# Splitting the output weight during the attention, loading the next stage's weights in its last heads, and moving the weighted sums ahead of the projections

## Chip, cores and metric

One NeuronCore of a Trainium2 chip runs the whole program. The metric is the device time of one execution in microseconds (us), smaller being better. The kernel before takes 3414.24 us, the median of three runs (3413.55 to 3415.07).

## What is computed

The reference is one transformer-like layer on x of shape 8 x 512 x 1024 in float32 (cut):

```python
x = x + attn_a(layernorm(x))      # qkv = x @ qkvw + qkvb; 32 heads of 32; softmax(q k^T * scale) v; ctx @ ow + ob
x = x + ffn(layernorm(x))         # dots = softmax(x @ centroids.T / 0.1); hits = dots > 0.01
                                  # dense = x @ weight.T + bias, kept where a row's query and its cluster are hit
x = x + attn_b(layernorm(x))      # 4 heads of 256, sign-bound q, k, v, causal sigmoid scores
x = x + ffn(layernorm(x))
```

Every float32 product is made of three float16 products: each operand is scaled by a power of two and split into a high half `hi` and a rest `lo`; hi·hi, hi·lo and lo·hi are added in PSUM. A projection of 128 rows onto 512 columns over 1024 features is thus a unit of 24 matmuls (8 blocks of features, 3 products each).

## The kernel before, in words

The program has four stages, each a block of five instruction streams (PE, DVE, ACT, POOL, SP) that are synchronised by semaphores, with a barrier (`end_phase`) between stages. SP issues nearly all DMAs, in its own order.

Stage 0 splits the qkv weight into `wqk` and `wv`, which fill the arena (48 parts of 2 KB per partition; `wqk` is parts 0 to 32, `wv` parts 32 to 48).

Stage 1 is attention A. It walks over 256 heads (8 rows of the batch x 32 heads) in **slots** `s`; four consecutive slots are one **group** `m` (64 groups). A slot has four **steps** `c`. In each step PE issues, in this order: one matmul of the row maxima of head s+2 (`max_scores`, L484, into `ring_ps`), one matmul of the scores of head s (`scores`, L494, into `st_ps`), in most steps a quarter of a projection unit, 6 matmuls (`unit`, L533 for q and k, L543 for v, into `proj_ps`), and one quarter of the weighted sum of head s-2 (`weighted`, 8 small matmuls, L511 and L514, into `ctx_ps`). I call a step with a quarter unit *full* and one without *empty*. A group has 12 full and 4 empty steps: the first unit sits in steps 0 to 3, the next in 5 to 8, the third in 10 to 13. So the first step of a group's second slot is empty. From slot 240 on there are no v units (two units in a group), and from slot 248 on no units at all.

The other engines: DVE takes the row maxima (L652), copies the finished sums out of `ctx_ps` (`leave_ctx`, L678 and L679, at the first step of a slot), and makes the rest `elo` of the exponentials of the first half of the keys (L670). ACT makes each exponential twice (L592 to float32, L598 to float16 `ehi`) and copies `proj_ps` out (L607, L610). POOL makes `elo` of the second half (L758), the normalised context (L766, L772) and the halves of the projections (L811, L813). ACT may overwrite `e32` of the second half only after POOL's L758 of the head before. SP sends the row of maxima to the partition where the scores read it (`rows`, L439, `qs<-nrow`), stores and restacks q and k, and stores the context of each group (L443).

The output weight `ow` (4 MB) is loaded at slot 240 by four DMAs (L461), after the last v unit has freed its arena parts and ahead of that slot's `rows`. In slots 242 to 249 DVE takes its maximum (L702), in slot 249 POOL reduces it over the partitions (`partition_all_reduce`, L834), and after the last head ACT makes `hi` (L644, 8 instructions) and DVE `lo` (L749, 8 instructions).

Stage 2 adds the projected context: for each of 32 tiles, `turn_context` (L999, 8 transposes), `hi_context` on ACT (L1078) and `lo_context` on DVE (L1249), two units `project` (L1011) and a residual. Ahead of tile 0 stands `project_bias` (L975, 48 matmuls, the value bias times the output weight), for which ACT spreads `bv_hl` (L1099), and whose result DVE adds to `obias` (L1137) after the centroids' scale. Here SP also loads the output bias, the centroids, the assignments, the ffn bias and the 4 MB of the ffn weight (L937 to L942), and POOL reduces the centroids' maximum (L1305) before its first `biases` (L1312). A second reduction for the ffn weight stands ten tiles later (L1330). Stages 3 and 4 are not touched.

Of the kernel before, what the change touches and what calls it, by code (L numbers as in the profile page):

```python
# [28 lines left out]
P = 128  # L29
# [16 lines left out]
GH = 4  # L46
NC = 64
# [80 lines left out]
def hybrid_layer(nc, x, qkvw, qkvb, ow, ob, bvq, bvk, bvv, fw, fb, cent, assign, out):  # L128
# [8 lines left out]

    ctx_d = nc.dram_tensor("ctx_scratch", (B * G, T, P, P), F32).ap()
# [12 lines left out]
    with ExitStack() as top:  # L151
# [19 lines left out]
        e_v = sb(top, "e_v", [P, 1])  # L171
        s_v = sb(top, "s_v", [P, 1])
        e_o = sb(top, "e_o", [P, 1])
        bv_hl = sb(top, "bv_hl", [P, 2, C], F16)
# [8 lines left out]
        wo = part16(0, 16).rearrange("p (a c n) -> p a c n", a=2, c=C)  # L183
        ow_raw = part32(32, 48).rearrange("p (c n) -> p c n", c=C)
# [3 lines left out]
        with ExitStack() as p01:  # L188
# [3 lines left out]
            exp_scale = sb(p01, "exp_scale", [P, 1])  # L192

# [93 lines left out]
            with ExitStack() as p1:  # L287
# [16 lines left out]
                ow_in = [sem(f"ow_in{i}") for i in range(4)]  # L304
                bvT_in, omax_done, oall_done, osc_done, wo_hi, wo_lo, bv_done = (sem(n) for n in (
                    "bvT_in", "omax_done", "oall_done", "osc_done", "wo_hi", "wo_lo", "bv_done"))
# [99 lines left out]
                with nc.Block() as block:  # L406

                    @block.sync
                    def _(sp):
# [34 lines left out]

                        for t in range(FIRST):
                            sp.dma_start(x_first(t), x_t[t // T, t % T]).then_inc(x0_in[t], 16)
# [4 lines left out]
                        for s in SLOTS:  # L451
# [6 lines left out]
                            if s == OW_LOAD:  # L458
                                sp.wait_ge(proj_full, place["V", B - 1, T - 1, 1] + 1)
                                for j in range(4):  # L460
                                    sp.dma_start(ow_raw[:, 2 * j:2 * j + 2], ow.rearrange("(c p) n -> p c n", p=P)[:, 2 * j:2 * j + 2]).then_inc(ow_in[j], 16)  # L461
                                with nc.allow_non_contiguous_dma(reason="a small bias, one feature per partition"):
                                    sp.dma_start(bvT[:], qkvb[2 * H:3 * H].rearrange("(c p) -> p c", p=P)).then_inc(bvT_in, 16)
                            if i == 1:
                                store_parts(m + 2, 0)
                            rows(s + 2)
                            if i == 2:
                                store_parts(m + 2, 1)
# [4 lines left out]
                        for i in range(2):  # L473
                            sp.wait_ge(ctx_out[i], 16 * GROUPS // 2)

# [71 lines left out]

# [1465 lines left out]
```

## Time and profile before

| | us |
|---|---|
| median of 3 runs | 3414.24 |
| the profiled execution's own time | 3413.33 |
| span of its instructions | 3411.6 |
| PE busy | 3211.6 (94%) |
| DVE busy | 2173.1 (64%) |
| POOL busy | 1864.7 (55%) |
| ACT busy | 1776.3 (52%) |

Times below are in us from the start of the span. Stage 1 ends at 1916.8, stage 2 reaches from there to 2368. "Idle before it" in square brackets is how long the engine stood still before an instruction, and what ended that. PE's matmuls are pipelined: of a row of matmuls the distance between starts is the cost, and the duration shown is longer (0.38 us for 512 columns whose starts are 0.22 us apart at full clock).

### The profile page before, as it was taken

What the parts mean: (1) busy time and instruction counts of PE and PEld (TensorE: products, weight loads), DVE (VectorE), ACT (ScalarE), POOL (GpSimd) and SP (SyncE); (2) the same over time, 40 slices, a digit from 0 to 9 for tenths busy, and PEclk for the clock granted to TensorE, in tenths of its full rate; (3) what the DMA queues carried; (4) which work ended last, traced back from release to release, by engine and by line L of the source; (5) the groups of instructions that cost most, each with busy time, mean ns of one, the idle gap of its engine ahead of it and who ended that gap; (6) DMA issues with size and microseconds to landing.
All of it is one profiled execution on the core that took longest, in us unless ns stands there. A gap on an engine that the chain in (4) does not pass through costs nothing. (4 is left out here: it accounts for less than half of the span.)

```text
span 3411.6 us, 62568 instructions
## 1 busy us (share of the span) xinstructions
PE 3211.6 (94%) x24256; PEld 1705.5 (50%) x24256; DVE 2173.1 (64%) x3858; ACT 1776.3 (52%) x2125; POOL 1864.7 (55%) x2065
## 2 busy tenths in 40 slices
PE   0899999999999999999997699998999999999999
PEld 0355555555555555555553355554455555554443
DVE  8377777777777777777777587775455555542311
ACT  3277777777777777777775422221345555552000
POOL 2377777777777777777664322221555555540422
PEclk9999999999999999999997799999999999999999
DMA  4122222222222222222223454443222222213533
GB/s 185 41 60 72 64 71 72 71 69 66 69 64 72 63 76 69 69 70 59 59 59 100 159 168 159 154 163 119 79 81 99 100 100 104 95 75 142 198 141 136
DMA packets 272869, 330.36 MB, mean 97 GB/s; under 512 B 91677, under 2 KB 206365, under 8 KB 271551
## 3 DMA queue, kind: packets, MB, share of 16 engines
q1 hardware_dynamic: 267902, 309.57, 28.6%
q10 hardware_dynamic: 4608, 16.78, 1.2%
q8 instruction: 194, 3.18, 0.4%
q14 instruction: 101, 0.82, 0.1%
q0 software_dynamic: 64, 0.01, 0.0%
HBM read 191.52 MB, written 134.22 MB: 95 GB/s over the span
## 5 line engine op out<-in xcount | busy, mean ns | idle before, releaser
L652 DVE TENSOR_REDUCE nmax<-ring_ps 128x1 f32<-128x512 f32 x1024 | 686.8, 688 | 417.4 <-PE ring_ps L484 414.0
L758 POOL TENSOR_TENSOR elo<-e,ehi 128x1024 f16<-128x1024 f32 x256 | 615.9, 2406 | 432.5 <-ACT ehi L598 425.1
L533 PE MATMUL proj_ps<-xnT,arena 128*128 128x512 f16 x3072 | 750.2, 380 | 3.3 <-DVE xnT L697 2.5
L592 ACT ACTIVATE e<-st_ps,exp_scale 128x1024 f32<-128x1024 f32 x512 | 571.4, 1116 | 344.3 <-PE st_ps L494 260.9
L598 ACT ACTIVATE ehi<-st_ps,exp_scale 128x1024 f16<-128x1024 f32 x512 | 570.1, 1114 | 64.7 <-PE ctx_ps L514 57.1
L533 PEld LDWEIGHTS proj_ps<-xnT,arena 128*128 128x128 f16 x3072 | 299.5, 98 | 373.0 <-ACT stage L610 10.6
L1527 PE MATMUL f_ps<-wT,fxT 128*128 128x512 f16 x1920 | 434.3, 380 | 2.9 <-DMA fxT<-xT_scratch 2.9
L494 PE MATMUL st_ps<-qs,ks 98*128 98x512 f16 x1024 | 396.8, 387 | 16.6 <-ACT ehi L598 10.0
L511 PEld LDWEIGHTS ctx_ps<-v_sb,ehi 128*128 128x128 f16 x4096 | 313.6, 98 | 192.8 <-DVE sums L679 81.5
L484 PE MATMUL ring_ps<-ks,qs 96*128 96x512 f16 x1024 | 401.1, 392 | 8.4 <-DVE nmax L652 8.2
L511 PE MATMUL ctx_ps<-v_sb,ehi 128*128 128x65 f16 x4096 | 374.6, 193 | 30.6 <-DVE sums L679 20.7
L543 PE MATMUL proj_ps<-arena,xnT 128*128 128x512 f16 x1536 | 371.4, 378 | 2.8 <-ACT stage L610 2.1
L514 PE MATMUL ctx_ps<-v_sb,elo 128*128 128x33 f16 x4096 | 359.6, 180 | 0.0
L1011 PE MATMUL o_ps<-arena,cT 128*128 128x512 f16 x1536 | 344.0, 381 | 6.2 <-DVE cT L1249 6.2
L514 PEld LDWEIGHTS ctx_ps<-v_sb,elo 128*128 128x128 f16 x4096 | 276.6, 97 | 111.2 <-issue 6.0
L670 DVE TENSOR_TENSOR elo<-e,ehi 128x1024 f16<-128x1024 f32 x256 | 322.7, 1261 | 0.9 <-ACT ehi L598 0.9
L1527 PEld LDWEIGHTS f_ps<-wT,fxT 128*128 128x128 f16 x1920 | 187.1, 98 | 207.8 <-issue 4.3
L543 PEld LDWEIGHTS proj_ps<-arena,xnT 128*128 128x128 f16 x1536 | 149.2, 97 | 187.0 <-ACT stage L610 3.5
L1011 PEld LDWEIGHTS o_ps<-arena,cT 128*128 128x128 f16 x1536 | 149.8, 98 | 175.4 <-DVE cT L1249 6.5
L1950 POOL TENSOR_TENSOR arena<-arena,fm 128x512 f32<-128x512 f32 x64 | 83.6, 1306 | 228.5 <-DVE fm L1803 228.5
L1320 POOL TENSOR_SCALAR rstd<-mv 128x1 f32<-128x1 f32 x32 | 7.2, 225 | 309.6 <-DVE mv L1198 302.7
L1810 DVE TENSOR_TENSOR h3T<-t_ps,h3T 128x512 f16<-128x512 f32 x64 | 44.3, 692 | 172.8 <-ACT h3T L1703 172.8
(238 smaller groups left out, 4655.9 us busy)
## 6 DMA issues: line engine op xcount, KB each, us to landing
qk_scratch<-qk_hl SPq DMA_DIRECT2D x128, 256.0 KB, 2.3
fxT<-xT_scratch SPq DMA_DIRECT2D x64, 512.0 KB, 3.5
qs<-qk_scratch SPq DMA_DIRECT2D x192, 128.0 KB, 2.7
ks<-qk_scratch SPq DMA_DIRECT2D x192, 128.0 KB, 2.9
arena<-x_scratch SPq DMA_DIRECT2D x48, 512.0 KB, 4.4
ctx_scratch<-ctx SPq DMA_DIRECT2D x64, 256.0 KB, 3.1
ct<-ctx_scratch SPq DMA_DIRECT2D x32, 512.0 KB, 4.8
xb<-in_L_attn_a_x_dram SPq DMA_DIRECT2D x32, 512.0 KB, 4.5
```

The costliest lines, as they stand in the source:

```text
L484: pe.matmul(ring_ps[:, ring_max(h, c) % 2, :], qs_v[0:3 * HD, h % RING, c, :], ks[0:3 * HD, h % RING, :], start=True, stop=True).then_inc( ...
L494: mm = pe.matmul(st_ps[:, c // 2, c % 2, :], ks[0:3 * HD + 2, h % RING, P * c:P * c + P], qs[0:3 * HD + 2, h % RING, :], start=True, stop= ...
L511: pe.matmul(ctx_v[:, t, :], ehi[:, h % 2, c, P * t:P * t + P], v_sb[:, c, hh, :], start=(c == 0 and t == 0), stop=False, skip_group_check= ...
L514: mm = pe.matmul(ctx_v[:, t, 0:HD + 1], elo[:, h % 2, c, P * t:P * t + P], v_sb[:, c, hh, 0:HD + 1], start=False, stop=(c == T - 1), skip_ ...
L533: mm = pe.matmul(proj_ps[:], wqk[:, wp, c, H * qk + P * g:H * qk + P * g + P], xnT[:, b % 2, xp, c, :], start=(n == 0), stop=(n == 23))
L543: mm = pe.matmul(proj_ps[:], xnT[:, b % 2, xp, c, P * t:P * t + P], wv[:, wp, c, S * half:S * half + S], start=(n == 0), stop=(n == 23))
L592: nc.scalar.activation(e32[:, half], st_ps[:, half], ACT.Exp, scale=exp_scale[:, 0:1]).then_inc(e32_done, 1)
L598: nc.scalar.activation(ehi[:, h % 2, 2 * half:2 * half + 2, :], st_ps[:, half], ACT.Exp, scale=exp_scale[:, 0:1]).then_inc(ehi_done, 1)
L652: dve.tensor_reduce(nmax[:, h % 2, c:c + 1], ring_ps[:, ring_max(h, c) % 2, :], AX.X, ALU.max, negate=True).then_inc(ring_free, 1)
L758: nc.gpsimd.tensor_tensor(elo[:, h % 2, 2:4, :], e32[:, 1], ehi[:, h % 2, 2:4, :], ALU.subtract).then_inc(elo_pool, 1)
L1011: mm = pe.matmul(o_ps[:, half, :], cT[:, n % 2, xp, c, :], wo[:, wp, c, 512 * half:512 * half + 512], start=(i == 0), stop=(i == 23))
L1527: pe.matmul(f_ps[:, half, :], fxT[:, t % 2, xp, c, :], wT[:, wp, c, cols], start=(n == 0), stop=False)
```

## The change

1. **Order on PE.** In steps 1 to 3 of a slot the weighted sum now stands ahead of the projection's quarter; in step 0 it stays behind.
2. **The output weight.** Its maximum is taken in slots 214 to 221 from 8 loads of 512 KB into the free tile `xt`; POOL's reduction stands in slot 222. In slots 223 to 239 each 512 KB piece is loaded again, ACT makes `hi` and DVE `lo` in `xt`, and SP stores both to a scratch tensor in DRAM. In slots 241 to 248 the halves are loaded from there into arena parts 32 to 48.
3. **The bias product.** Its 48 matmuls are two units in slots 251 and 253, and DVE adds them to `obias` in slots 252 and 254. `project_bias` and its helpers leave stage 2.
4. **Loads of stage 2.** The output bias, the first context tile (`ct0`), centroids, assignments, ffn bias and the ffn weight (8 x 512 KB) are loaded in slots 249 to 256. At the end of stage 1 SP waits for them.
5. **Start of stage 2.** The work on the centroids moves behind the first tile's; POOL's reduction stands behind its first two `biases`. Tile 0's context needs no load.

Its core, in the order of the file: the plan of slots, SP's `out_weight` (called in each slot behind `rows(s + 2)`), PE's order, the work of ACT, DVE and POOL, and what changes at the start of stage 2 on PE and POOL.

```diff
+    wo_d = nc.dram_tensor("wo_scratch", (C, P, 2, H), F16).ap()
-        wo = part16(0, 16).rearrange("p (a c n) -> p a c n", a=2, c=C)
-        ow_raw = part32(32, 48).rearrange("p (c n) -> p c n", c=C)
+        wo = part16(32, 48).rearrange("p (a c n) -> p a c n", a=2, c=C)
+        kq, signs, obias, cst, asg, asgf, ct0, fbx = (part32(2 * i, 2 * i + 2) for i in range(8))
...
-                OW_LOAD = GH * (GROUPS - 4)
-                OW_MAX = OW_LOAD + 2
-                OW_SCALE = OW_MAX + C
+                OW_MAX = GH * (turn_group(B * T - 1) + 2)
+                OW_SCALE = OW_MAX + C + 3
+                OW_SPLIT = OW_SCALE
+                WO_LOAD = OW_SPLIT + 2 * C + 2
+                REST = WO_LOAD + C
+                BIAS = REST + 2
+                for half in range(2):
+                    for q in range(4):
+                        fills.setdefault((BIAS + 2 * half, q), []).append((("B", half), 6 * q, 6 * q + 6))
...
+                        def out_weight(s):
+                            j = s - OW_MAX
+                            if 0 <= j < C:
+                                sp.wait_ge(proj_full, place["T", B * T - 2 + j % 2, 1] + 1)
+                                wait(sp, omax_done, j - 1)
+                                sp.dma_start(xt[:, j % 2], ow_c[j]).then_inc(ow_in[j % 2], 16)
...
+                            if not odd and 1 <= c <= C:
+                                sp.wait_ge(wo_lo, c)
+                                sp.dma_start(wo_d[c - 1], halves).then_inc(wo_out, 16)
+                            if not odd and 0 <= c < C:
+                                sp.wait_ge(omax_done, C)
+                                wait(sp, wo_lo, c)
+                                sp.dma_start(raw, ow_c[c]).then_inc(raw_in, 16)
+                            c = s - WO_LOAD
+                            if 0 <= c < C:
+                                sp.wait_ge(proj_full, place["V", B - 1, T - 1, 1] + 1)
+                                sp.wait_ge(wo_out, 16 * C)
+                                sp.dma_start(wo[:, :, c], wo_d[c]).then_inc(wo_in, 16)
+                            c = s - REST
+                            if 0 <= c < C:
+                                sp.wait_ge(proj_full, place["QK", GROUPS - 1, 1] + 1)
...
+                                sp.dma_start(fw_raw[:, c], fw_o[c]).then_inc(fw_in, 16)
...
-                            if s == OW_LOAD:
-                                sp.wait_ge(proj_full, place["V", B - 1, T - 1, 1] + 1)
-                                for j in range(4):
-                                    sp.dma_start(ow_raw[:, 2 * j:2 * j + 2], ow.rearrange("(c p) n -> p c n", p=P)[:, 2 * j:2 * j + 2]).then_inc(ow_in[j], 16)
...
                                 max_scores(s + 2, c)
                                 scores(s, c)
+                                if c:
+                                    weighted(s - 2, c)
                                 for f in fills.get((s, c), []):
-                                    unit(*f)
-                                weighted(s - 2, c)
+                                    if f[0][0] == "B":
+                                        bias_unit(*f)
+                                    else:
+                                        unit(*f)
+                                if c == 0:
+                                    weighted(s - 2, c)
...
-                        for c in range(C):
-                            nc.scalar.activation(wo[:, 0, c, :], ow_raw[:, c, :], ACT.Copy, scale=so[:, 0:1]).then_inc(wo_hi, 1)
+                                j, odd = (s - OW_SPLIT - 1) // 2, (s - OW_SPLIT - 1) % 2
+                                if c == 3 and not odd and 0 <= j < C:
+                                    out_weight_hi(j)
...
-                                if c == 2 and OW_MAX <= s < OW_SCALE:
-                                    out_weight_max(s - OW_MAX)
+                                if c == 1 and 0 <= s - OW_MAX - 2 < C:
+                                    out_weight_max(s - OW_MAX - 2)
+                                j, odd = (s - OW_SPLIT - 2) // 2, (s - OW_SPLIT - 2) % 2
+                                if c == 0 and not odd and 0 <= j < C:
+                                    out_weight_lo(j)
...
-                                if c == 3 and s == OW_SCALE - 1:
+                                if c == 1 and s == OW_SCALE - 1:
                                     pool.wait_ge(omax_done, C + 1)
                                     nc.gpsimd.partition_all_reduce(m2o[:], m1o[:], P, RMAX).then_inc(oall_done, 1)
...
-                        project_bias()
                         turn_context(0)
...
-                        pool.wait_ge(max2, 1)
-                        nc.gpsimd.partition_all_reduce(m2[:, 1:2], m1[:, 1:2], P, RMAX).then_inc(all2, 1)
-                        pool.wait_ge(ob_done, 2)
...
                             biases(k + 1)
+                            if k == 0:
+                                pool.wait_ge(max2, 1)
+                                nc.gpsimd.partition_all_reduce(m2[:, 1:2], m1[:, 1:2], P, RMAX).then_inc(all2, 1)
```

PE, from a full step through the empty first step of a group's second slot. Before:

```order
152 L533 MATMUL proj_ps<-xnT,arena 128x512 x6
153 L511 MATMUL ctx_ps<-v_sb,ehi 128x65
154 L514 MATMUL ctx_ps<-v_sb,elo 128x33
155 L511 MATMUL ctx_ps<-v_sb,ehi 128x65
156 L514 MATMUL ctx_ps<-v_sb,elo 128x33
157 L511 MATMUL ctx_ps<-v_sb,ehi 128x65
158 L514 MATMUL ctx_ps<-v_sb,elo 128x33
159 L511 MATMUL ctx_ps<-v_sb,ehi 128x65
160 L514 MATMUL ctx_ps<-v_sb,elo 128x33
161 L484 MATMUL ring_ps<-ks,qs 128x512
162 L494 MATMUL st_ps<-qs,ks 128x512
163 L511 MATMUL ctx_ps<-v_sb,ehi 128x65
```

The same place of the change (L563 and L566 are the weighted sum, L585 the projection, L536 and L546 maxima and scores):

```order
154 L563 MATMUL ctx_ps<-v_sb,ehi 128x65
155 L566 MATMUL ctx_ps<-v_sb,elo 128x33
156 L563 MATMUL ctx_ps<-v_sb,ehi 128x65
157 L566 MATMUL ctx_ps<-v_sb,elo 128x33
158 L563 MATMUL ctx_ps<-v_sb,ehi 128x65
159 L566 MATMUL ctx_ps<-v_sb,elo 128x33
160 L585 MATMUL proj_ps<-xnT,arena 128x512 x6
161 L536 MATMUL ring_ps<-ks,qs 128x512
162 L546 MATMUL st_ps<-qs,ks 128x512
163 L563 MATMUL ctx_ps<-v_sb,ehi 128x65
```

The six projection matmuls have moved between the last quarter of one head's weighted sum and the first quarter of the next one's.

POOL, around the reduction of the output weight's maximum. Before (slot 249; an `ISA` row without a tile is a switch of POOL's code), and then the change (slot 222; L859 is `elo`, L867 and L873 the context, L912 and L914 the halves of a projection):

```order
1346 L758 TENSOR_TENSOR elo<-e,ehi 128x1024
1347 L766 TENSOR_TENSOR sums<-sums 128x4x32
1348 L772 TENSOR_TENSOR ctx<-sums,rsum 128x4x32
1349 L834 ISA
1350 L834 ISA m2o<-m1o 128x1
1351 L758 ISA
1352 L758 TENSOR_TENSOR elo<-e,ehi 128x1024
```

```order
1231 L873 TENSOR_TENSOR ctx<-sums,rsum 128x4x32
1232 L935 ISA
1233 L935 ISA m2o<-m1o 128x1
1234 L912 CAST qk_hl<-stage 128x512
1235 L914 ISA
1236 L914 TENSOR_TENSOR qk_hl<-stage,qk_hl 128x512
1237 L859 TENSOR_TENSOR elo<-e,ehi 128x1024
```

The two switches are still there, but between the reduction and the next `elo` there is now also a projection to be split.

PE at the start of stage 2, before and in the change (L1076 transposes the context, L1086 projects):

```order
11033 L975 MATMUL o_ps<-arena,xT 128x512 x48
11034 L999 MATMUL t_ps<-ident,ct 128x128 x8
11035 L1011 MATMUL o_ps<-arena,cT 128x512 x24
11036 L999 MATMUL t_ps<-ident,ct 128x128 x8
11037 L966 MATMUL c_ps<-ident,xn 128x64 x8
```

```order
11039 L1076 MATMUL t_ps<-ident,arena 128x128 x8
11040 L1086 MATMUL o_ps<-arena,cT 128x512 x24
11041 L1076 MATMUL t_ps<-ident,ct 128x128 x8
11042 L1053 MATMUL c_ps<-ident,arena 128x64 x8
11043 L1086 MATMUL o_ps<-arena,cT 128x512 x48
```

The 48 matmuls of the bias are gone from the head of the stage.

## Rows read from the trace of the kernel before

**Rows 1.** Busy time by stretch: length, then each engine, PEclk, DMA share, GB/s

```profile
500.00:1000.00 500.00, 494.08 (x4328) 260.39 (x4326) 374.83 (x689) 370.40 (x377) 369.56 (x395) 1.00 0.25 68
1791.60:1897.40 105.80, 76.70 (x691) 39.08 (x689) 77.65 (x145) 66.37 (x64) 55.22 (x54) 0.77 0.28 83
1937.00:2368.00 431.00, 421.14 (x2880) 239.42 (x2878) 317.57 (x570) 96.45 (x209) 99.45 (x97) 0.99 0.47 159
```

**Rows 2.** PE's waits over the whole run: us in total, times, longest

```profile
PE ctx_ps L511 <- DVE sums L679: 20.7, 37, 2.1
PE st_ps L494 <- DMA qs<-nrow: 6.5, 2, 6.1
```

**Rows 3.** Timeline of PE, two slots of group 18, and the last such place

```profile
650.25 0.39 PE L484 MATMUL ring_ps<-ks,qs 96*128 96x512 f16 x1
...
652.21 0.39 PE L484 MATMUL ring_ps<-ks,qs 96*128 96x512 f16 x1
652.44 0.38 PE L494 MATMUL st_ps<-qs,ks 98*128 98x512 f16 x1
652.96 0.20 PE L511 MATMUL ctx_ps<-v_sb,ehi 128*128 128x65 f16 x1
...
1770.63 0.20 PE L511 MATMUL ctx_ps<-v_sb,ehi 128*128 128x65 f16 x1
```

**Rows 4.** Timeline of DVE at the same place

```profile
652.40 0.18 DVE L678 RECIPROCAL rsum<-ctx_ps 128x4 f32<-128x4 f32 x1 [0.57 <-PE ctx_ps L514]
```

**Rows 5.** Timeline of DVE, two slots without projections; then its groups, 1800 to 1900

```profile
1887.13 0.18 DVE L678 RECIPROCAL rsum<-ctx_ps 128x4 f32<-128x4 f32 x1
1891.72 0.17 DVE L678 RECIPROCAL rsum<-ctx_ps 128x4 f32<-128x4 f32 x1
...
L702 DVE TENSOR_REDUCE mxo<-arena 128x1 f32<-128x1024 f32 x8 | 9.7, 1209 | 0.0
```

**Rows 6.** Timeline of ACT: first exponential of slots 240 and 255, and after POOL's reduction

```profile
1791.70 1.11 ACT L592 ACTIVATE e<-st_ps,exp_scale 128x1024 f32<-128x1024 f32 x1 [0.87 <-DVE elo L670]
...
1877.17 1.11 ACT L592 ACTIVATE e<-st_ps,exp_scale 128x1024 f32<-128x1024 f32 x1 [10.61 <-POOL elo L758]
...
1897.43 1.13 ACT L592 ACTIVATE e<-st_ps,exp_scale 128x1024 f32<-128x1024 f32 x1
```

**Rows 7.** Timeline of PE at the two long stalls before slot 250

```profile
1810.00 0.61 PE L494 MATMUL st_ps<-qs,ks 98*128 98x512 f16 x1 [6.08 <-DMA qs<-nrow]
...
1879.35 0.61 PE L494 MATMUL st_ps<-qs,ks 98*128 98x512 f16 x1 [6.74 <-ACT ehi L598]
```

**Rows 8.** DMA issues from 1794 to 1812: count, KB each, us to landing

```profile
arena<-in_L_attn_a_attn_ow_dram SPq DMA_DIRECT2D x4, 1024.0 KB, 10.2
ctx_scratch<-ctx SPq DMA_DIRECT2D x1, 256.0 KB, 3.6
```

**Rows 9.** Timeline of POOL: two reductions, each with the work behind it

```profile
1867.18 0.38 POOL L834 PARTITION_ALL_REDUCE m2o<-m1o  x1 [5.83 <-issue]
1874.97 2.11 POOL L758 TENSOR_TENSOR elo<-e,ehi 128x1024 f16<-128x1024 f32 x1 [7.41 <-issue]
...
2077.10 0.38 POOL L1330 PARTITION_ALL_REDUCE m<-m  x1 [7.49 <-issue]
2084.35 0.25 POOL L1320 TENSOR_SCALAR rstd<-mv 128x1 f32<-128x1 f32 x1 [6.88 <-issue]
```

**Rows 10.** Timelines of ACT, DVE and SP at the end of stage 1

```profile
1901.87 8.41 ACT L644 ACTIVATE arena<-arena,so 128x1024 f16<-128x1024 f32 x8
...
1905.63 10.12 DVE L749 SCALAR_TENSOR_TENSOR arena<-arena,so 128x1024 f16<-128x1024 f32 x8
...
1908.72 0.37 SPq L443 DMA_DIRECT2D ctx_scratch<-ctx  x1
```

**Rows 11.** Timeline of PE at the start of stage 2

```profile
1929.70 1.04 PE L999 MATMUL t_ps<-ident,ct 128*128 128x128 f32 x8
1936.59 5.72 PE L1011 MATMUL o_ps<-arena,cT 128*128 128x512 f16 x15 [5.85 <-DVE cT L1249]
```

More of the change, by code:

```diff
@@ L546, in unit, with bias_unit @@
                                 mm.then_inc(proj_full, 1)
+                        def bias_unit(u, a, z):
+                            half = u[1]
+                            if a == 0 and half == 0:
+                                pe.wait_ge(proj_free, len(order))
+                                pe.wait_ge(bvx_hi, 1)
+                                pe.wait_ge(bvx_lo, 1)
+                                pe.wait_ge(wo_in, 16 * C)
+                            elif a == 0:
+                                pe.wait_ge(ob_done, 1)
+                            for n in range(a, z):
+                                c, (xp, wp) = n // 3, ((0, 0), (0, 1), (1, 0))[n % 3]
+                                mm = pe.matmul(proj_ps[:], bvx[:, xp, c, :], wo[:, wp, c, S * half:S * half + S],
+                                               start=(n == 0), stop=(n == 23))
+                            if z == 24:
+                                mm.then_inc(bias_full, 1)
                         def turn_first(t):
@@ L621, in normalise_x, with out_weight_hi @@
                                                  bias=shift[:, n % 2:n % 2 + 1]).then_inc(xn_done, 1)
+                        def out_weight_hi(c):
+                            act.wait_ge(osc_done, 3)
+                            act.wait_ge(raw_in, 16 * (c + 1))
+                            wait(act, wo_out, 16 * c)
+                            nc.scalar.activation(halves[:, 0], raw, ACT.Copy, scale=so[:, 0:1]).then_inc(wo_hi, 1)
                         for t in range(T):
@@ L967, in turn_centroids @@
                             mm.then_inc(c_turned, 1)
-                        def project_bias():
-                            pe.wait_ge(bv_hi, 1)
-                            pe.wait_ge(bv_lo, 1)
-                            for half in range(2):
-                                for i in range(24):
-                                    c, (xp, wp) = i // 3, ((0, 0), (0, 1), (1, 0))[i % 3]
-                                    mm = pe.matmul(o_ps[:, half, :], xT[:, 0, xp, c, :], wo[:, wp, c, 512 * half:512 * half + 512],
-                                                   start=(i == 0), stop=(i == 23))
-                                mm.then_inc(bv_full, 1)
                         def turn_weights(k):
@@ L992, in turn_context @@
                                 return
[L993 removed]
+                            wait(pe, ct_in[n % 3], 16 * (n // 3 + 1 if n % 3 else n // 3))
+                            src = ct[:, n % 3] if n else ct0
                             wait(pe, w_lo, min(n - 1 - W_FIRST, 2 * C))
```

154 lines of the change are left out of this document (85 added, 69 removed).

## Prediction

> **What bounds the kernel now.** I read the busy time by stretch first [rows 1]. From 500 to 1000, in the middle of attention A, PE is busy 494 of 500 us at full clock, with DVE, ACT and POOL near 370 each: PE is the bound, and only PE's work or its gaps can be saved there. Stage 2 is the same: 421 of 431. The exception is the end of stage 1: from 1791.60 to 1897.40 PE is busy 76.7 of 105.8 us, with a granted clock of 0.77. Then I read PE's waits [rows 2], and the timelines at the waits, where the starts of matmuls tell more than the busy sum does.
>
> The steady part first. A full step takes 1.96 us (652.21 less 650.25, rows 3); the eight matmuls of 512 columns in it start 0.22 apart, the weighted quarter takes the rest. An empty step would take 3 x 0.22 = 0.66. In the first step of a group's second slot, the scores start at 652.44 and the weighted sum at 652.96 [rows 3]: 0.52 instead of 0.22, a **gap of 0.30 us**. DVE explains it [rows 4]: its reciprocal at 652.40 had idled 0.57 for PE's last weighted quarter, which stood behind six projection matmuls, and PE's next weighted sum waits for the copy behind that reciprocal. The same gap stands in each of 59 groups, the last at 1770.63 [rows 3]. The sum of PE's waits counts 20.7 us in 37 waits [rows 2], since it sees only what exceeds a matmul's own tail.
>
> The late slots: without projections two reciprocals are 4.59 apart [rows 5], with DVE busy throughout, so DVE bounds an empty slot at 4.6 (PE needs 2.65). Two stalls lie in this stretch: PE waits 6.08 for `qs<-nrow` at 1810.00 [rows 2, 7], behind four 1 MB loads of the output weight that take 10.2 to land [rows 8], and ACT waits 10.61 for POOL's `elo` at 1877.17 [rows 6], since POOL's reduction costs 5.83 before and 7.41 behind it, besides its own 0.38 [rows 9]. The restart is slow, too: the scores' matmul is shown with 0.61 after the first stall [rows 7] against 0.38 in mid attention [rows 3], which is the level of 1.2 GHz against 2.4.
>
> **The change, part by part.** Against the profiled execution's own 3413.3 (0.9 below the median).
>
> (a) *Weighted sums ahead of projections.* In the full step before the gap, PE's last weighted quarter now comes 6 x 0.22 = 1.3 us earlier. DVE had idled 0.57 for it, so it is ready 0.57 earlier, and PE's wait of 0.30 goes, with 0.27 to spare. No instruction is added. 59 x 0.30 = **-18**. Bounds: 0 (DVE late for another reason) and -18. What is late next is DVE itself, 0.27 behind. The projection's copy-out starts 0.2 later, and PE wants that bank again one empty step later at the soonest (0.66 plus 0.6 of other matmuls), so this costs nothing.
>
> (b) *Slots 240 to 254.* Before: 1897.43 less 1791.70 = 105.7 [rows 6]. After: the load of the weight, the eight maxima (1.21 each in DVE-bound slots, rows 5) and POOL's reduction are gone from here. Groups 60 and 61: one slot of four full steps (7.84), one of three full and one empty (6.54), two at DVE's 4.6, so 23.6 each, 47.2. Then seven slots: five at 4.6 and two that hold a bias unit and are PE-bound at 4 x 1.96 = 7.84, so 38.7. Together 85.9. PE idles in the empty slots, and part of this will run at the lower clock: 48 bias matmuls at half clock would cost 10.4 more, none 0; I take 4. 89.9 - 105.7 = **-16**, bounds -20 and -8. The 16 loads of 512 KB here take, at 10.2 per 4 MB, 1.3 each in slots of 4.6 or more, and stand behind `rows`: nothing.
>
> (c) *End of stage 1.* DVE's eight `lo` end at 1905.63 + 10.12 = 1915.75 [rows 10], and stage 2 starts 1.05 later. ACT's eight `hi` (8.41) lie ahead of them. Without both, the last store of the context sets the end: issued at 1908.72 [rows 10], landing 3.6 later [rows 8], plus 1.05: 1913.4. POOL's last steps could be faster without DVE beside them (nothing to 2 us). **-4.5**, bounds -3 and -6.
>
> (d) *Start of stage 2.* Before: the stage starts at 1916.8, the first projection at 1936.59 [rows 11]. After: `ct0` is in place, PE transposes at once (1.04 at full clock, 2 at half), ACT and DVE copy both halves: from the transposes' end at 1930.74 to the projection would have been 2 without the bias ahead on DVE. So it starts about 4 after the stage does: 19.8 - 4 = **-16**, bounds -12 and -17. POOL's reduction now stands behind two `biases`; with its switches it holds POOL some 14 us, and the first tile's `rstd` comes near 25 after the stage's start instead of 20. PE has 48 projection matmuls of the second tile to do meanwhile (10.4), and wants the first normalised tile only near 29: nothing. The scratch copy adds nothing here.
>
> (e) *POOL's reduction in slot 222*, in the PE-bound part. POOL is away 5.83 + 0.38 + 7.41 = 13.6 [rows 9], and a projection's split stands ahead of the next `elo`. Its 10.61 at ACT [rows 6] was met with slots of 4.6; slots of 6.6 leave about 2 us more slack. PE lost 6.74 in one wait at 1879.35 then, and most of 10 over the slot. I take 8.5 of stall and 2 for the clock behind it: **+10.5**, bounds +5 and +15. What waits behind: splits, the restack and the context of POOL; each has a slot or more of slack. The Trainium skill (GPSIMD Engine Reference, Instruction dispatch) gives about 6 us for the first call of freshly loaded code, with no visible instruction. The trace agrees at 5.83, but it also shows 7.41 and, elsewhere, 7.49 before and 6.88 behind [rows 9]; by the page's figure for both switches the term would be 1 us smaller.
>
> (f) *Sixteen DVE and eight ACT instructions in slots 214 to 239.* A maximum is 1.21, a `lo` 10.12 / 8 = 1.27, a `hi` 8.41 / 8 = 1.05 [rows 5, 10]. DVE and ACT idle a quarter of this stretch [rows 1], but unevenly: in a slot with two empty steps (5.3) DVE's 4.6 plus 1.3 overflow by 0.6. Eight such places at up to 0.5: **+2**, bounds 0 and +10. In DMA: 24 transfers of 512 KB, one or two a slot, 1.3 each, behind `rows`.
>
> Sum: -18 - 16 - 4.5 - 16 + 10.5 + 2 = **-42**, so 3371.3 for such an execution and 3372 for the median.
>
> **Rivals.**
> *Mid attention is out of balance (17%).* Each of the 24 added instructions costs its share of a bubble because ACT's exponentials, DVE's copy-out and POOL follow one another. For it: DVE is 0.27 from being late even after (a), and POOL's times stretch beside DVE. Against: a quarter of idle time. With (f) at +10 and (e) at +15: 3385.
> *The order brings nothing (8%).* Another wait takes the gap's place: 3390. For it: DVE's chain of maxima, row parts and copy-out is only 0.27 short. Against: its idle of 0.57.
> *The clock (12%).* The stall in slot 224 and the empty slots keep PE at 1.2 GHz through both bias units: +10.4, so 3382. For it: 0.77 granted in this stretch [rows 1]. The Trainium skill (TensorE: Matmul & The Clock Gate, HAM oscillation) says that idle gaps between bursts bring the clock back to half, and speaks against moving a stall into dense work; the durations of rows 7 agree.
> *Slower than before (3%).* The row transfers queue behind the new ones: there are 40 transfers of 512 KB (8 loads for the maximum, 8 for the split, 8 stores, 8 loads back, 8 of the ffn weight). If `qs<-nrow` waits for one in front of it each time, as it did for 4 MB at 1810.00, PE loses 10.2 / 8 = 1.3 each: 52, so 3424. It decides once a row's transfer lands later than a slot after its issue. Against: `rows` is issued first and has 6.6 us.
> That the change does not do what it says: the order of each engine shows that it does.
>
> **How the numbers follow.** My forecast (3362 to 3379) has 60%. The range of 3358 to 3391 takes in the three rivals that are still faster. A measurement of this kernel can tell 0.2% (7 us) from no change: faster by more than that 95%, within it 2% (a share of the rivals that end just below), slower 3%.
>
> **What would show it.** Per step: (a) no PE wait for `sums` in a group's second slot and 0.30 less per group; (b) slots 240 to 254 in about 90 us; (c, d) stage 2's first projection about 4 after its start, which comes about 3 after the last context store's landing; (e) one PE wait of 6 to 10 us near slot 224; (f) short PE waits for `sums` or `nmax` in slots 214 to 239, at most 0.5 each. PE waits for `qs<-nrow` would refute it, and so would a period in mid attention that stays.

## Result and the profile after

The changed kernel takes 3385.36 us (median of 4 runs, 3383.96 to 3387.10), the kernel before on the same chip 3413.89 (4 runs, 3413.21 to 3415.07). The ratio is 0.9918, with a 95% interval of [0.9906, 0.9931]: 28.5 us faster. I had forecast 42. The profiled execution took 3387.1 us with a span of 3385.3, against 3413.3 and 3411.6 before, so 26.3 of the difference lie in the spans. One of the five executions of experiment 4 took 3979.20 us at a granted clock of 0.80, against 0.99 in the others, and is left out of its range and ratio.

The stretches come first: mid attention, slots 240 to 254, and stage 2. Columns as in [rows 1].

```profile
500.00:1000.00 500.00, 495.38 (x4335) 263.22 (x4334) 380.48 (x694) 361.80 (x377) 387.05 (x394) 1.00 0.24 69
1804.40:1891.90 87.50, 78.32 (x732) 41.45 (x729) 69.37 (x132) 66.00 (x65) 55.13 (x53) 0.90 0.56 162
1908.00:2340.00 432.00, 420.57 (x2880) 238.26 (x2880) 320.35 (x579) 96.15 (x209) 100.34 (x98) 0.99 0.47 157
```

The late slots take 87.5 instead of 105.8 us [rows 1], at a granted clock of 0.90 instead of 0.77. In mid attention PE is as busy as before, with seven more matmuls in the 500 us. ACT's first exponentials of slots 216, 240 and 255, and stage 2's first projection, divide the program (in us):

| stretch | before | after | difference | forecast |
|---|---|---|---|---|
| start to slot 216 | 1631.1 | 1626.3 | -4.7 | -16 (a) |
| slots 216 to 239 | 160.6 | 178.0 | +17.4 | +10.7 (rest of a, e, f) |
| slots 240 to 254 | 105.7 | 87.5 | -18.2 | -16 (b) |
| slot 255 to stage 2's first projection | 39.2 | 16.5 | -22.7 | -20.5 (c, d) |
| the rest | | | +2.0 | 0 |

**Slots 216 to 239.** PE's waits over the whole run (us in total, times, longest):

```profile
PE ring_ps L536 <- DVE nmax L735: 17.0, 25, 1.3
PE ctx_ps L563 <- DVE sums L762: 12.7, 32, 1.4
PE st_ps L546 <- ACT ehi L672: 11.3, 8, 7.6
PE t_ps L1076 <- PEq L163: 5.4, 1, 5.4
```

The wait of 6.08 for `qs<-nrow` [rows 2, 7] is gone, and no new one for DMA stands in its place. There are now waits for the row maxima `nmax` of up to 1.3 us, and one of 7.6 for `ehi`. The latter is POOL's reduction. The timelines of POOL, ACT and PE in the kernel after show it:

```profile
1675.31 0.38 POOL L935 PARTITION_ALL_REDUCE m2o<-m1o  x1 [5.88 <-issue]
...
1683.21 1.14 POOL L914 TENSOR_TENSOR qk_hl<-stage,qk_hl 128x512 f16<-128x512 f32 x1 [6.98 <-issue]
1684.33 2.11 POOL L859 TENSOR_TENSOR elo<-e,ehi 128x1024 f16<-128x1024 f32 x1
```

```profile
1686.81 1.11 ACT L666 ACTIVATE e<-st_ps,exp_scale 128x1024 f32<-128x1024 f32 x1 [9.98 <-POOL elo L859]
```

```profile
1688.98 0.61 PE L546 MATMUL st_ps<-qs,ks 98*128 98x512 f16 x1 [7.56 <-ACT ehi L672]
1689.76 2.72 PE L585 MATMUL proj_ps<-xnT,arena 128*128 128x512 f16 x6
```

5.88 before and 6.98 behind a 0.38 us instruction are what the kernel before had, too, at 5.83 and 7.41 [rows 9]. Behind the stall six matmuls take 2.72 instead of 1.46 us: the granted clock is 0.50 from 1689.8 to 1693.4.

**Mid attention.** The wait that (a) meant to remove is gone, and another has come. PE and ACT of the kernel after, in the fourth slot of a group that turns an x tile:

```profile
694.36 0.38 PE L536 MATMUL ring_ps<-ks,qs 96*128 96x512 f16 x1
...
695.00 0.18 PE L566 MATMUL ctx_ps<-v_sb,elo 128*128 128x33 f16 x1
695.21 0.66 PE L632 MATMUL proj_ps<-ident,xt 128*128 128x128 f32 x4
```

```profile
694.56 0.60 ACT L684 ACTIVATE stage<-proj_ps 128x512 f32<-128x512 f32 x1 [0.41 <-PE proj_ps L595]
```

The four transposes (L632) want `proj_ps` back one empty step after the v unit's last quarter, but ACT's copy of it (L684) starts at 694.56 and takes 0.60. They start 0.21 after the small matmul in front of them instead of 0.03.

**Start of stage 2.** PE of the kernel after:

```profile
1905.04 1.94 PE L1076 MATMUL t_ps<-ident,arena 128*128 128x128 f32 x8 [5.39 <-PEq L163]
1908.39 7.70 PE L1086 MATMUL o_ps<-arena,cT 128*128 128x512 f16 x24 [1.41 <-DVE cT L1315]
```

The first projection starts 3.4 us after the stage does, instead of 19.8 [rows 11].

### The profile page after: what moved, and what is told of

Same layout as the page of the kernel before. It is cut to its first block and busy times, and to the rows that moved or that the text cites. A ratio compares the mean times of both kernels' runs of the same rounds, so it can differ in the third digit from the quotient of the medians.

```text
span 3385.3 us, 62616 instructions
## 1 busy us (share of the span) xinstructions
PE 3205.6 (95%) x24256; PEld 1711.9 (51%) x24256; DVE 2189.8 (65%) x3858; ACT 1745.6 (52%) x2125; POOL 1927.5 (57%) x2065
## 5 line engine op out<-in xcount | busy, mean ns | idle before, releaser
L735 DVE TENSOR_REDUCE nmax<-ring_ps 128x1 f32<-128x512 f32 x1024 | 676.2, 685 | 418.2 <-PE ring_ps L536 415.6
L859 POOL TENSOR_TENSOR elo<-e,ehi 128x1024 f16<-128x1024 f32 x256 | 669.6, 2616 | 355.7 <-ACT ehi L672 355.7
L585 PE MATMUL proj_ps<-xnT,arena 128*128 128x512 f16 x3072 | 750.5, 381 | 3.3 <-DVE xnT L780 2.5
L585 PEld LDWEIGHTS proj_ps<-xnT,arena 128*128 128x128 f16 x3072 | 272.3, 97 | 286.9 <-ACT stage L684 11.7
L536 PE MATMUL ring_ps<-ks,qs 96*128 96x512 f16 x1024 | 397.2, 388 | 17.0 <-DVE nmax L735 17.0
L546 PE MATMUL st_ps<-qs,ks 98*128 98x512 f16 x1024 | 392.6, 383 | 12.0 <-ACT ehi L672 11.3
L563 PEld LDWEIGHTS ctx_ps<-v_sb,ehi 128*128 128x128 f16 x4096 | 312.5, 97 | 155.1 <-DVE sums L762 39.3
L563 PE MATMUL ctx_ps<-v_sb,ehi 128*128 128x65 f16 x4096 | 372.0, 192 | 14.0 <-DVE sums L762 12.7
L566 PE MATMUL ctx_ps<-v_sb,elo 128*128 128x33 f16 x4096 | 355.8, 179 | 0.0
L1086 PE MATMUL o_ps<-arena,cT 128*128 128x512 f16 x1536 | 344.0, 381 | 3.2 <-DVE cT L1315 3.2
L753 DVE TENSOR_TENSOR elo<-e,ehi 128x1024 f16<-128x1024 f32 x256 | 333.3, 1302 | 1.1 <-ACT ehi L672 1.1
L566 PEld LDWEIGHTS ctx_ps<-v_sb,elo 128*128 128x128 f16 x4096 | 274.7, 97 | 116.1 <-issue 3.1
L1086 PEld LDWEIGHTS o_ps<-arena,cT 128*128 128x128 f16 x1536 | 149.8, 98 | 172.9 <-DVE cT L1315 4.0
L595 PEld LDWEIGHTS proj_ps<-arena,xnT 128*128 128x128 f16 x1536 | 135.4, 97 | 144.0 <-ACT stage L684 3.5
L536 PEld LDWEIGHTS ring_ps<-ks,qs 96*128 96x128 f16 x1024 | 115.8, 113 | 97.4 <-DVE nmax L735 34.5
```

The costliest lines, as they stand in the source:

```text
L536: pe.matmul(ring_ps[:, ring_max(h, c) % 2, :], qs_v[0:3 * HD, h % RING, c, :], ks[0:3 * HD, h % RING, :], start=True, stop=True).then_inc( ...
L546: mm = pe.matmul(st_ps[:, c // 2, c % 2, :], ks[0:3 * HD + 2, h % RING, P * c:P * c + P], qs[0:3 * HD + 2, h % RING, :], start=True, stop= ...
L563: pe.matmul(ctx_v[:, t, :], ehi[:, h % 2, c, P * t:P * t + P], v_sb[:, c, hh, :], start=(c == 0 and t == 0), stop=False, skip_group_check= ...
L566: mm = pe.matmul(ctx_v[:, t, 0:HD + 1], elo[:, h % 2, c, P * t:P * t + P], v_sb[:, c, hh, 0:HD + 1], start=False, stop=(c == T - 1), skip_ ...
L585: mm = pe.matmul(proj_ps[:], wqk[:, wp, c, H * qk + P * g:H * qk + P * g + P], xnT[:, b % 2, xp, c, :], start=(n == 0), stop=(n == 23))
L595: mm = pe.matmul(proj_ps[:], xnT[:, b % 2, xp, c, P * t:P * t + P], wv[:, wp, c, S * half:S * half + S], start=(n == 0), stop=(n == 23))
```

## Experiments

Each is a ratio to the kernel before on the same chip, over five rounds. The first two put a price on the new order of PE, one in each kernel.

**1. The order alone.** The kernel before, with only this:

```diff
                                 scores(s, c)
+                                if c:
+                                    weighted(s - 2, c)
                                 for f in fills.get((s, c), []):
                                     unit(*f)
-                                weighted(s - 2, c)
+                                if c == 0:
+                                    weighted(s - 2, c)
```

> The kernel before with nothing changed but PE's order (weighted sums ahead of the projection in steps 1 to 3). My theory now: each group's 0.30 us gap before the weighted sum goes, but the four transposes of a tile, which stand first in step 3 of a group's last slot, now wait about 0.25 us for ACT's copy-out of the v unit, in 52 groups. So about 3413.9 - 59 x 0.30 + 52 x 0.25 = 3409, 3405 to 3411. The prediction's term (a) says 3396. The rival that the order is worth nothing says 3413 to 3415.

Measured: 3409.79 (3405.78 to 3412.53), ratio 0.9987 [0.9978, 0.9995]: 3.9 us, not 18.

**2. The change without the new order.** The change, with `weighted(s - 2, c)` behind the fills in every step.

> The changed kernel with PE's old order back. If the order is worth 5 us as in the trace of the change: 3385.4 + 5 = 3390, with a gap of 0.30 us in each group's second slot again and no wait of the transposes. If it is worth the 18 us of term (a), and something else ate 13 of it, 3403. If the order also shifts when POOL's stall or the split's waits hit PE, it may end below 3385.

Measured: 3392.77 (3390.78 to 3395.18), ratio 0.9936 [0.9924, 0.9948]: the order is worth 7.4 us in the change. In the traces the first exponentials of slot 216 come 3.3 us earlier by the order in experiment 1 and 4.3 earlier in the change. Both runs refute 18. I counted, for each place in a group, by how much the distance between two starts of PE exceeds the median for that kind of instruction (slots 0 to 211, us in total):

| place | old order (2) | change |
|---|---|---|
| second slot, step 0: scores to weighted sum | 52 x 0.30 = 15.6 | 0 |
| first slot, step 0, alternate groups: units to weighted sum | 14.7 | 12.9 |
| fourth slot: small matmul to transposes | 0 | 52 x 0.20 = 10.2 (50 of 0.19, two of 0.4) |
| among those transposes | 1.8 | 2.9 |
| second slot, step 1: unit to maxima, alternate groups | 0 | 24 x 0.10 = 2.4 |
| fourth slot, step 1: unit to maxima | 0 | 1.6 |

The gap did go. It came back at the transposes and, in small pieces, before the maxima. The rows add up to 32.1 and 30.0 us. The slots shrank by a little more, some 4 us, because most full steps are also shorter by up to 0.01 us each.

**3. One step in sixteen back.** The change, with the fills first again in the step in which the v unit ends:

```diff
-                                if c:
+                                ahead = c and (s % GH, c) != (3, 1)
+                                if ahead:
                                     weighted(s - 2, c)
...
-                                if c == 0:
+                                if not ahead:
                                     weighted(s - 2, c)
```

> The changed kernel, but in one step of a group, the second of its last slot, the projection's quarter stays ahead of the weighted sum as before, so that the copy-out has 0.2 us more before the transposes. Theory: the transposes' wait of 0.25 us goes in 52 groups, 13 us at most, the first gap stays away: 3385.4 - 12 = 3373. Rival: the wait is DVE's or moves to the next step: 3383 to 3387.

Measured: 3378.10 (3376.66 to 3379.19), ratio 0.9893 [0.9877, 0.9908]: 7.3 us faster than the change, where I had expected 12. Its timelines of PE and ACT at the same place:

```profile
690.31 0.39 PE L536 MATMUL ring_ps<-ks,qs 96*128 96x512 f16 x1
...
690.98 0.64 PE L632 MATMUL proj_ps<-ident,xt 128*128 128x128 f32 x4
```

```profile
690.28 0.60 ACT L685 ACTIVATE stage<-proj_ps 128x512 f32<-128x512 f32 x1 [0.18 <-PE proj_ps L595]
```

ACT's copy starts 0.03 before the step's first matmul instead of 0.20 behind it, and the transposes 0.67 behind that matmul instead of 0.85. In the count above, the 10.2 falls to 0.8 and the 2.9 to 1.9. The wait of alternate groups in the first slot rises from 12.9 to 15.7 and takes part of it back.

**4. The subtraction later.** In the change, DVE's `lo` of the output weight (L803) stands at step 0, behind the maximum, and idles there for ACT's `hi` (L701). Here it stands behind the maximum of step 2.

```diff
-                                if c == 0 and not odd and 0 <= j < C:
+                                if c == 2 and not odd and 0 <= j < C:
                                     out_weight_lo(j)
```

> The changed kernel with DVE's low halves of the output weight two steps later in the same slot. Theory: in slots 225 to 239 DVE stood 1.6 us waiting for ACT's high half and then took 1.27 us, so that the row maxima came late and PE waited 1.25 and 0.8 us in turn, plus 0.2 in the next slot: some 9 us in eight slots. Two steps later ACT is done, so the idle part goes: 3385.4 - 6 = 3379, at best 3377. Rival (DVE's sheer load is the cost, not its wait): no change, 3384 to 3387.

Measured: 3388.45 (3386.42 to 3389.38), ratio 0.9923 [0.9909, 0.9936]: no gain. DVE and ACT show two new costs:

```profile
1772.83 1.28 DVE L803 SCALAR_TENSOR_TENSOR xt<-xt,so 128x1024 f16<-128x1024 f32 x1
...
1774.74 1.08 DVE L743 SCALAR_TENSOR_TENSOR nrow<-nmax,zero 128x4 f16<-128x4 f32 x1
...
1776.34 2.92 DVE L753 TENSOR_TENSOR elo<-e,ehi 128x1024 f16<-128x1024 f32 x1
```

```profile
1770.33 1.15 ACT L701 ACTIVATE xt<-xt,so 128x1024 f16<-128x1024 f32 x1 [1.65 <-DMA xt<-in_L_attn_a_attn_ow_dram]
```

The `lo` is quick now (1.28), but `elo` behind it takes 2.92. In slots 225 to 239 eight of DVE's `elo` take 2.0 or 2.9 us, where all sixteen took 1.22 in the change, and ACT's exponentials wait 13.5 us for them instead of 4.1. (The 1.08 on 128x4 is no new cost: that instruction takes up to 1.10 in the change.) And since the block's buffer is reloaded only once `lo` has read it, ACT waits once, 1.65 us, for a block's DMA, ahead of its exponentials. Slots 225 to 239 take 109.3 us instead of 106.2.

**5. Without the subtraction.** In seven of eight blocks `lo` covers two columns (left out: the low part of seven blocks).

> After the change, with VectorE's subtraction of the output weight's low part cut to two columns in seven of its eight blocks (left out: the low part of seven blocks, which the products then take from block 0). Theory (VectorE's own work is what is too much in slots 225 to 239: 1.86 to 2.22 us for each subtraction, behind which its maxima wait): the groups there fall from 28.47 to about 26.7 us, and the time from 3385 by 4 x 1.8 to about 3378. Rival 1 (ScalarE's conversion of the high part, 1.15 us ahead of its exps, is what is too much): the groups stay at 28 or more, 3383 to 3386. Rival 2 (both, each in half): about 3381.

Measured: 3381.49 (3377.26 to 3382.35), ratio 0.9903 [0.989, 0.9917]. The first exponentials of slots 228 and 232, in the change and here:

```profile
1718.93 1.11 ACT L666 ACTIVATE e<-st_ps,exp_scale 128x1024 f32<-128x1024 f32 x1 [1.03 <-DVE elo L753]
...
1747.39 1.11 ACT L666 ACTIVATE e<-st_ps,exp_scale 128x1024 f32<-128x1024 f32 x1 [1.03 <-DVE elo L753]
```

```profile
1719.55 1.11 ACT L666 ACTIVATE e<-st_ps,exp_scale 128x1024 f32<-128x1024 f32 x1 [0.81 <-DVE elo L753]
...
1746.26 1.11 ACT L666 ACTIVATE e<-st_ps,exp_scale 128x1024 f32<-128x1024 f32 x1 [0.73 <-DVE elo L753]
```

A group takes 28.46 in the change and 26.71 without the subtraction: 1.75 less. Slots 225 to 239, where the seven shortened blocks lie, take 100.3 instead of 106.1, 5.8 less, and before the change they took 100.2. The theory of DVE holds in these slots, and ACT's `hi` alone costs next to nothing. The profiled span fell by 4.7, since slots 223 and 224 with their stall were 0.9 longer here; the medians fell by 3.9, less than the 7 I had expected, which had counted four whole groups.

**6. The maximum without POOL.** The change, with the reduction over partitions made by one matmul and a DVE maximum:

```diff
...
+                                if (s, c) == (OW_SCALE, 2):
+                                    pe.wait_ge(omax_done, C + 1)
+                                    pe.wait_ge(proj_free, place["QK", GROUP_R + 2, 0])
+                                    pe.matmul(proj_ps[:, 0:P], m1o[:, 0:1].to_broadcast([P, P]), ident[:],
+                                              start=True, stop=True).then_inc(omax_full, 1)
...
+                                if (s, c) == (OW_SCALE, 3):
+                                    dve.wait_ge(omax_full, 1)
+                                    dve.tensor_reduce(m2o[:], proj_ps[:, 0:P], AX.X, ALU.max).then_inc(oall_done, 1)
...
-                                    nc.gpsimd.partition_all_reduce(m2o[:], m1o[:], P, RMAX).then_inc(oall_done, 1)
```

> After the change, with GpSimd's reduction over partitions replaced by one 128x128 matmul into the bank of the projections in an empty step of slot 223 and a maximum by VectorE. Theory (the reduction stalls the pipeline 7.7 us and leaves 3.9 us at half clock): 3385 - 11.6 = about 3374, and no stall of more than 1.5 us before slot 240. Rival (the stall goes, but the low clock has another cause or VectorE's added wait takes its place): 3377 to 3380.

Measured: 3375.92 (3374.78 to 3380.29), ratio 0.9894 [0.9878, 0.9909]: 9.4 us faster than the change. From the first exponentials of slot 223 to those of 225 it is 16.0 instead of 24.5 us, and from slot 216 to slot 240 it is 169.5 instead of 178.0. The new instructions:

```profile
1675.38 0.46 PE L665 MATMUL proj_ps<-ident,m1o 128*128 128x128 f32 x2
```

```profile
1675.88 0.29 DVE L843 TENSOR_REDUCE m2o<-proj_ps 128x1 f32<-128x128 f32 x1 [0.33 <-PE proj_ps L665]
```

**7. Without the bias products.** The bias units of slots 251 and 253 and DVE's addition are left out (and with them the V bias's part of the output).

> After the change, without the bias products in slots 251 and 253 and without VectorE's addition of them (left out: the product of the V bias with the output weight). Theory (the bias is partly in the shadow of ScalarE's exps, slots 251 and 253 take 6.54 and 6.18 us where their neighbours without it take 4.0 to 4.9): 3 to 5 us less, about 3381. Rival (it is on the path in full, 48 matmuls x 0.2155): 10.3 less, 3375.

Measured: 3383.25 (3380.86 to 3384.96), ratio 0.991 [0.9897, 0.9924]: 2.1 us faster than the change. In its trace slots 251 and 253 take 4.92 and 4.58 instead of 6.54 and 6.18, so 3.2 us for 10.3 us of matmuls: most of them fill what PE would have idled.

**8. The subtraction in halves** of 512 columns, behind the maxima of steps 1 and 2.

> After the change, with VectorE's subtraction in two halves of 512 columns, behind the maxima of steps 1 and 2, in place of one of 1024 behind that of step 0. Theory (both the wait of 1.27 us for ScalarE at step 0 and the length of one piece count, since the ring of maxima is two banks deep): the gap of 1.25 us in the first slot of each pair goes, the other stays, 3 to 5 us less, about 3381. Rival (VectorE's load beside GpSimd's is what counts, wherever it is put): no gain, 3384 to 3388, as with the subtraction two steps later.

Measured: 3394.97 (3394.43 to 3398.30), ratio 0.9948 [0.9935, 0.996]: 9.6 us slower than the change, worse than either theory. Its timelines of DVE and POOL say why:

```profile
1761.39 1.68 DVE L805 SCALAR_TENSOR_TENSOR xt<-xt,so 128x512 f16<-128x512 f32 x1 [0.67 <-ACT xt L701]
...
1766.20 2.05 DVE L746 SCALAR_TENSOR_TENSOR nrow<-nmax,nrow 128x4 f16<-128x4 f32 x1
```

```profile
1760.40 2.13 POOL L862 TENSOR_TENSOR elo<-e,ehi 128x1024 f16<-128x1024 f32 x1 [4.09 <-ACT ehi L672]
...
1766.10 2.12 POOL L862 TENSOR_TENSOR elo<-e,ehi 128x1024 f16<-128x1024 f32 x1
```

DVE's subtraction on 128x4, which takes 0.16 elsewhere, starts 0.1 behind POOL's `elo` and ends at 1768.25, when POOL's ends (1768.22). The half block ends at 1763.07, 0.54 after POOL's `elo`. So two pieces can meet POOL twice, and push the row parts and the copy of the sums into its time, too.

**9. ACT's part earlier.** The change, with `hi` behind step 2 of its slot instead of step 3.

> After the change, with ScalarE's conversion of the high part two half-slots ahead (behind step 2 instead of step 3 of the slot), where its record shows 1.5 us of idle time before the exps; VectorE's subtraction stays behind the maximum of step 0. Theory (with VectorE's subtraction in place the loss is its wait of 1.27 us for ScalarE in front of its own 1.3 us, the maxima that wait behind both): the gaps of 1.25 and 0.78 us before the maxima of slots 225 to 239 go or fall below 0.3, the groups fall from 28.47 to about 26.8, 3378. Rival (VectorE's load alone, as where the subtraction was moved behind step 2): the groups stay above 28, 3384 to 3387.

Measured: 3387.59 (3385.00 to 3388.64), ratio 0.9921 [0.9906, 0.9935]: nothing, and SP and ACT show what the edit overlooked:

```profile
1763.12 0.38 SPq L479 DMA_DIRECT2D xt<-in_L_attn_a_attn_ow_dram  x1
```

```profile
1768.24 1.15 ACT L701 ACTIVATE xt<-xt,so 128x1024 f16<-128x1024 f32 x1 [3.74 <-DMA xt<-in_L_attn_a_attn_ow_dram]
```

The block lands 5.1 us after its issue, so ACT stands 3.74 us in front of it, with its exponentials behind (18.5 us in six waits). DVE's waits for `hi` fell from 7.2 to 2.0 us, and PE's 6.9 us of waits for `nmax` in slots 225 to 239 are gone, but 6.4 us of waits for ACT's `ehi` stand there instead. The split is a ring of load, `hi` and `lo` through one buffer, in step with pairs of slots. The time did not decide between wait and load.

**10 and 11. Edits together.** First experiments 3, 6 and 9, then 3 and 6.

> The change with three edits together: the fills ahead of the weighted sums again in step 1 of the fourth slot of a group, the maximum of the output weight by TensorE and VectorE, ScalarE's conversion behind step 2. Theory (they add up: 7.3, 9.5 and up to 7): 3361 to 3369. Rival (the earlier conversion brings nothing): 3369.

> The change with two edits together: the fills ahead of the weighted sums again in step 1 of the fourth slot of a group, and the maximum of the output weight by TensorE and VectorE. Theory (they lie in different stretches and add up, 7.3 and 9.5): about 3369. Rival (part of one is lost with the other): 3371 to 3376.

Measured: 3373.78 (3372.56 to 3376.19), ratio 0.988 [0.9864, 0.9897], and 3373.51 (3369.52 to 3373.80), ratio 0.9878 [0.9863, 0.9892]. The edit of experiment 9 adds nothing. By the medians the two gains of 11 add up only in part (11.9 of 16.7), as its rival said. In the trace of 11 PE stands still for 2.9 us in slot 224, waiting for DVE's copy of the sums, and DVE and POOL show what holds the copy up:

```profile
1670.67 2.12 DVE L809 TENSOR_TENSOR bv_hl<-bvs,bv_hl 128x8 f16<-128x8 f32 x1
...
1672.81 0.39 DVE L772 COPY sums<-ctx_ps 128x260 f32<-128x260 f32 x1
```

```profile
1670.65 2.12 POOL L872 TENSOR_TENSOR elo<-e,ehi 128x1024 f16<-128x1024 f32 x1 [1.21 <-ACT ehi L682]
```

A subtraction on 128x8, which took 0.17 in the change, starts 0.02 behind POOL's `elo` and lasts as long.

**12. The subtraction one step later**, on top of 11: behind the maximum of step 1.

> As the version with two edits (fills first in one step of a group, maximum by TensorE and VectorE), and VectorE's subtraction behind the maximum of step 1 instead of step 0. Theory A (what costs is VectorE's idle wait for ScalarE at step 0, and behind step 1 it has the next two steps as slack): the groups of slots 224 to 239 fall from 28.47 to about 27.3, 3373.5 - 4 = 3369. Theory B (VectorE's reads of SBUF stand still while GpSimd works, so a subtraction that comes later pushes the row parts and the copy of the sums into GpSimd's time, as in the run with halves, where groups took 31.3): the groups stay at 28.5 to 30, 3373 to 3379.

Measured: 3367.99 (3363.24 to 3371.09), ratio 0.9864 [0.9847, 0.988]: what theory A said (3369), and the best version: 17.4 us below the change and 45.8 below the kernel before. Its interval overlaps that of 11, so the two traces have to say whether the last edit counts. Slots 225 to 239, by busy time, in the change and here:

```profile
1698.20:1804.35 106.15, 99.06 (x866) 51.20 (x865) 89.48 (x143) 77.88 (x79) 79.35 (x70) 1.00 0.40 120
```

```profile
1685.35:1786.05 100.70, 98.86 (x867) 52.29 (x866) 86.82 (x142) 77.19 (x79) 81.03 (x70) 1.00 0.42 127
```

It takes 100.7 with all the work, against 106.2 in the change and 106.1 in 11; experiment 5, where the work was missing, takes 100.3. PE's waits for `nmax` in these slots are 1.6 us (none above 0.2), against 6.9 in the change and 5.7 in 11 (up to 1.1 each), which is the gain. Yet its subtraction still meets POOL and idles for ACT:

```profile
1739.54 2.22 DVE L813 SCALAR_TENSOR_TENSOR xt<-xt,so 128x1024 f16<-128x1024 f32 x1 [0.67 <-ACT xt L711]
```

DVE ends it when it did, 2.25 us after ACT's `hi`, but two maxima are done ahead of it instead of one, so that PE, two banks of maxima ahead, has something to do.

## Why the prediction was partly right

The direction and the wide range (3358 to 3391) held. The forecast itself (3362 to 3379, given 60%) did not, and the median missed by 13: -28.5 instead of -42. Two terms carry the miss, (a) and (f); the others were within about 2 us each.

(a) *-18 forecast; -3.9 alone and -7.4 in the change.* This is the step that failed. DVE's part was right: the wait of 0.30 in the second slot vanished at every place. The failing sentence is the last: the copy-out "starts 0.2 later, and PE wants that bank again one empty step later at the soonest (0.66 plus 0.6 of other matmuls), so this costs nothing". The 0.2 was right. But the transposes stand at the head of the next step, and the 0.66 already holds all the matmuls of the empty one. So from 0.20 a copy of 0.60 ends at 0.80 and cannot be done by 0.66. Experiment 3 shows that this step carried most of it: with the copy's 0.2 us back in one step of sixteen, 10.2 us of the wait fell to 0.8. My rival "the order brings nothing" said that another wait would take the gap's place, which is what happened, but it looked for that wait in DVE's chain. I had named DVE as the next one late, with 0.27 to spare, and not looked for the other users of the moved work.

(f) *+2 forecast, bounds 0 and +10; about +9.* It was under-sized. Without POOL's reduction slots 216 to 239 take 169.5 us (6), against 160.6 in the kernel before. Of this 8.9, the `lo` of slots 225 to 239 are about 6 (5.8 for seven of the eight in experiment 5); the other 3 lie in slots 223 and 224, and no run takes them apart. I had priced each instruction by its duration and DVE's mean idle time. What counted was its place: a `lo` at step 0 begins 1.27 late, behind ACT, takes 2.22 beside POOL, and the maxima behind it feed PE through two banks only. Moved by one step it cost next to nothing (12), by two steps 3.2 us more than at first (4), in two pieces more still (8). My rival on the balance of mid attention said this, and its (f) of +10 was close. That its 3385 is where the time came out is luck: it put 4.5 more on (e), where there were none, and the missing gain was (a)'s.

(e) *+10.5 forecast; 9.4 by the medians of 6, 8.5 by its slots 216 to 239.* The stall of 7.6 and the half clock behind it came where I had put them, in slots 223 and 224. Behind this stall the granted clock is 0.50, the lower of the two levels, and six matmuls take 2.72 us. The Trainium skill (TensorE: Matmul & The Clock Gate, HAM oscillation) says that TensorE starts slow again after such an idle wait; the trace agrees.

(b) *-16 forecast; -18.2.* The slots took 87.5, not 89.9. The bias units were over-priced: I made slots 251 and 253 PE-bound at 7.84, and they take 6.54 and 6.18; without the units they take 4.92 and 4.58 (7). Part of the agreement is luck: slots 240 to 243 took 27.3 where I had added up 23.6, which used up most of the 4 I had put on the clock.

(c) *and* (d) *-20.5 forecast; -22.7.* From the first exponentials of slot 255 to the stage's start it is 6.3 less (forecast 4.5), and from there to the first projection 3.4 us where I said about 4.

The rivals of the clock through both bias units and of queued row transfers did not come: the granted clock of slots 240 to 254 is 0.90, and PE waits for none of the 40 added transfers, and for a row transfer only once, 0.4 us at the start of attention. (The clock rival's price was also too high by its own sum: (b) already held 4 of its 10.4, so it should have said 3378 and not 3382.)

Left open: the +2.0 in the rest of the program, and the 3 us of (f) in slots 223 and 224.

## What to carry to other kernels

When an instruction moves ahead of another, follow the one it passed, too: who copies its result out, who wants that buffer next, and at which instruction of the step, counted in starts. A bubble removed from a tight pipeline goes to the next user unless that one has slack.

Work added to a helper engine is priced by its place between two deliveries, not by its duration and the mean idle time. One step's shift took 5.4 us from its stretch here (12 against 11), and two steps' added 3.2 (4 against the change). And a rare instruction that idles its engine for 5.9 us before it and 7.0 behind it is worth replacing by two on engines that are there anyway.

## What the hardware showed that I had not expected

*DVE and POOL can shut each other out for a whole instruction.* DVE's subtractions on 128x4 and 128x8 took 2.05 and 2.12 instead of 0.16 and 0.17 and ended with POOL's `elo` (experiments 8 and 11). In the change the same is seen at L803:

```profile
1755.29 2.22 DVE L803 SCALAR_TENSOR_TENSOR xt<-xt,so 128x1024 f16<-128x1024 f32 x1 [1.27 <-ACT xt L701]
```

```profile
1754.30 2.13 POOL L859 TENSOR_TENSOR elo<-e,ehi 128x1024 f16<-128x1024 f32 x1 [4.10 <-ACT ehi L672]
1756.39 1.38 POOL L867 TENSOR_TENSOR sums<-sums 128x128 f32<-128x128 f32 x1
```

POOL's `elo` ends at 1756.43, DVE's `lo` 1.08 later, and POOL's sum of the context, 0.40 elsewhere, ends 0.26 behind that. The row maxima, whose one operand lies in PSUM, take between 0.67 and 0.69 in all 1024 cases of the change. The Trainium skill (SBUF — State Buffer, SBUF: two separate sides) says that a VectorE instruction with two SBUF inputs and a GpSimd instruction that reads SBUF lock a shared pair of ports, and that the later one waits for all of the earlier. These rows agree. So the duration of such an instruction in a profile is partly waiting, and moves with the phase between the two engines.

*A 128x128 float32 matmul against the identity, with the column of maxima spread over its weights, spreads the maxima over all partitions*: 0.46 us on PE and 0.29 for the maximum on DVE, in place of 13.2 us of POOL (5.88 + 0.38 + 6.98).
